# Attention probabilities of even steps: turned by VectorE and a round trip through DRAM instead of by TensorE

## The chip, the cores and the metric

One core of a Trainium2 chip runs the whole program in one launch. The metric is the device time of one execution in microseconds, from the first instruction to the last landing; of several executions the median counts.

## What is computed

The program is one layer: cross-attention with a tanh gate, then a mixture of experts with a tanh gate, both behind a layer norm and both added to `x`. The change lies inside the attention alone. Cut to that (32 sequences of 64 rows, width 512; 32 query heads of 128 in 8 groups that share a key and value head; float32 throughout):

```python
q = rmsnorm((layernorm(x) @ Wq.T).reshape(B, 64, 32, 128), q_norm_w)
k = rmsnorm((ctx @ Wk.T).reshape(B, 64, 8, 128), k_norm_w)      # each shared by 4 query heads
v = (ctx @ Wv.T).reshape(B, 64, 8, 128)
scores = einsum('bhqd,bhkd->bhqk', q, k) / sqrt(128) + mask
probs = softmax(scores)
x = x + tanh(g_xattn) * (einsum('bhqk,bhkd->bhqd', probs, v) @ Wo.T)
```

The product of the probabilities with the values sums over the key positions `k`. TensorE sums over partitions, and the scores come out with the queries on the partitions. So each block of probabilities has to be turned, queries and keys exchanged, before that product.

## The kernel before

**Tiling.** The attention runs in `STEPS` = 64 steps: 8 groups of heads, and in each group 8 steps of 256 rows (4 sequences). A step holds 4 heads x 4 sequences. Its scores are one tile of 128 partitions (2 heads x 64 queries) by 8 blocks of 64 keys. Steps go in pairs; with `i = 2 * d + odd` a step is even or odd, and the two kinds differ in their order of work. Matmuls take float32 numbers as a high part and a rest (`_hi`, `_lo`), three matmuls for one product (`split_product`, L607): the high part is copied out of PSUM by ScalarE, the rest is subtracted by VectorE.

**Who does what in step i.** Each engine has a list of its own, written out by hand, in loops over pairs of steps, and works through it strictly in order; semaphores tie the lists together.

- TensorE (`step`, L777): queries of step i+1 for two halves of the heads (`q_head`, L681); the product of the probabilities of step i-1 with the values (`probs_v`, L731); scores of step i+1 (`scores`, L690); the turn of step i's probabilities (`transpose_probs`, L722: four 128x128 turns against the identity); then the output product of earlier steps (`outputs`, L763, which calls `project_out`, L713, and between its halves `add_quarters`, L708, a small product that completes the sums of the squared queries). In an odd step the turn stands inside the second half of the queries, goes to PSUM banks 2 and 3, and its start is the line `if odd` (L792). In an even step it stands behind the scores (L804) and goes to bank 6. That bank is also written by the first output product, so `outputs` waits there until the turned tile has been read (L771).
- ScalarE (`act_step`, L1201): copies of the queries (`q_out`) and their squares (`squares`), the high part of the turned probabilities (`probs_hi`, L1179), the high part of the attention output (`a_hi_tile`, L1188), the high part of the next group's weight slice (`split_slice`, L1196), and the exponentials of step i+1's softmax (`exps`, L1169).
- VectorE (`dve_step`, L1613): 32x32 block turns and sums of the squared queries (`turn_squares` L1520, `sum_squares` L1529, `split_sums` L1535), the rest of the attention output (`a_rest`, L1513), the rest of the turned probabilities (`probs_lo`, L1589), the softmax of step i+1 (`softmax`, L1544), the addition of the output products into the accumulator (`add_out`, L1506, which stands inside the softmax, while it waits for others), and the rest of the weight slice (`slice_lo`, L1598; for both steps of a pair it stands in the odd one).
- GpSimd: the inverse root of the squared query sums (L500) and the split of the values (`split_v`, L502).
- SP issues the loads (`next_loads`, L370): in each step a slice of 512 columns of weights (L378) and the next values (L384), in each odd step the keys of the next pair (L336). It, too, waits in order.

`softmax` writes the probabilities into the one tile `pb`; its last two passes (L1587) count `p_ready`. The high parts and rests of the turned probabilities go to the tiles `pt`, columns 0 to 127 for even steps and 128 to 255 for odd ones.

The steps 0 to 3 are written out, and so are the last 8 (in the last group other work is mixed in). The loops of the three groups' pairs between them are real loops; each engine jumps back at their ends.

Of the kernel before, what the change touches and what calls it, by code (L numbers as in the profile page):

```python
# [51 lines left out]
STEPS = KVH * NC  # L52
TURNED = (3, STEPS - NC)
# [13 lines left out]
def build(nc, x, ctxT, wk, wv, w_att, w_shd, mask, g_x, g_f, q_w, k_w, gate, w_gu, w_dn, out):  # L67
    kbuf = nc.dram_tensor("kbuf", [STEPS, P, CT], F32, kind="Internal").ap()
    vbuf = nc.dram_tensor("vbuf", [STEPS, P, CT], F32, kind="Internal").ap()
# [3 lines left out]
    k_pair = kbuf.rearrange("(d c) p n -> d p c n", c=2)  # L73
    k_st = kbuf.rearrange("(g c) p (b t) -> c b p g t", g=KVH, b=2)
# [4 lines left out]
    with ExitStack() as ctx:  # L79
# [145 lines left out]
        oh2 = sb("oh2", [P, NT, E])  # L225
        sgt = [sb(f"sgt{q}", [P, D]) for q in range(1)]
# [30 lines left out]
        sq_turned, sq_part, fold_ok = sem("sq_turned"), sem("sq_part"), sem("fold_ok")  # L257
# [10 lines left out]
        tri_ok, rank_out = sem("tri_ok"), sem("rank_out")  # L268
# [17 lines left out]
        dve_mark, pool_mark, ones_ok = sem("dve_mark"), sem("pool_mark"), sem("ones_ok")  # L286
        ctx_first = [sem("ctx_first0"), sem("ctx_first1")]

        block = ctx.enter_context(nc.Block())

# [20 lines left out]
        def _(sp):  # L311

            for s in (v_stored, k_stored, *h2_stored, wgu_last):
                sp.sem_inc(s, 16)
# [55 lines left out]
            def next_loads(d, odd, x_tiles=()):  # L370

                i = 2 * d + odd
                if odd:
                    sp.wait_ge(s_done, i + 1)
                    load_k(d + 1)
                sp.wait_ge(w_hi, i + 8)
# [6 lines left out]
                sp.wait_ge(v_split, 2 * i + 2)  # L383
                sp.dma_start(vt[:].rearrange("p b t -> p (b t)"), vbuf[i + 1]).then_inc(vt_in, 16)  # L384

            with sp.Fori(0, (STEPS - NC) // 2) as d:
                for odd in range(2):
                    next_loads(d, odd)

# [77 lines left out]
        def _(pool):  # L467

            pool.memset(onesb[:], 1.0).then_inc(ones_ok, 1)
            pool.memset(mhalf[:], -0.5).then_inc(pool_const, 1)  # L470
            pool.memset(ident[:], 0.0).then_inc(ident_ok, 1)
            pool.wait_ge(ident_ok, 1)
# [29 lines left out]
            def split_v(j):  # L502
                pool.wait_ge(vt_in, 16 * j + 16)
                pool.wait_ge(pv_done, 2 * j + 2)
                pool.sem_inc(pool_mark, 1)
# [51 lines left out]
            def split_down(z):  # L557
                cs = slice(256 * z, 256 * z + 256)
                pool.wait_ge(shd_in, 16)
                pool.sem_inc(pool_mark, 1)  # L560
# [53 lines left out]
        def _(pe):  # L614
            pe.wait_ge(ones_ok, 1)
            for z in range(WARM):
                pe.matmul(PS[7][:, 0:P], onesb[:], onesb[:], start=(z == 0), stop=(z == WARM - 1))
            pe.wait_ge(ident_ok, 2)
# [144 lines left out]
            def outputs(r, w_before, w_o, o_ready=None, turn=True):  # L763
# [53 lines left out]
            def opening():  # L817
# [29 lines left out]
                pe.wait_ge(fold_ok, 5)  # L847
# [124 lines left out]
            pe.wait_ge(tri_ok, 1)  # L972
# [111 lines left out]
        def _(act):  # L1084
# [94 lines left out]
            def probs_hi(i, odd, bank=2):  # L1179
                act.wait_ge(pT_done, i + 1)  # L1180
# [20 lines left out]
            def act_step(d, odd, w, sl):  # L1201
                i = 2 * d + odd
                act.wait_ge(s_done, i + 1)
                q_out(0, i + 1)
                squares(0, i + 1)
                if odd:
                    probs_hi(i, 1)
# [5 lines left out]
                a_hi_tile(i - 1, 1)  # L1213
                split_slice(i, w, sl)
                exps(i + 1)
# [42 lines left out]
            act.wait_ge(const_dve, 2)  # L1258
# [136 lines left out]
        def _(dve):  # L1395
# [13 lines left out]
            def row_statistics(n, tt):  # L1409
# [3 lines left out]
                dve.sem_inc(dve_mark, 1)  # L1413
# [83 lines left out]
            dve.wait_ge(ident_ok, 2)  # L1497
            dve.tensor_reduce(fold1[:], ident[:].rearrange("p (a j) -> p j a", a=4), AX, ALU.add).then_inc(fold_ok, 1)
            dve.tensor_reduce(quarter[:], ident[:].rearrange("p (a j) -> p a j", a=4), AX, ALU.add).then_inc(fold_ok, 1)
            dve.wait_ge(fold_ok, 2)  # L1500
            dve.tensor_copy(fold[:], fold1[:].unsqueeze(1).to_broadcast([P, 4, 32])).then_inc(fold_ok, 2)
# [42 lines left out]
            def softmax(j, *meanwhile):  # L1544
# [7 lines left out]
                else:  # L1552
                    if j is TURNED[0]:
                        dve.wait_ge(fold_ok, 5)
# [11 lines left out]
                dve.wait_ge(s_done, j + 1)  # L1566
                dve.tensor_tensor(pb[:], PS[3][:].rearrange("p (b s) -> p b s", s=S), per_row(qr),
# [21 lines left out]
            def probs_lo(i, odd, bank=2):  # L1589
                if odd:  # L1590
                    for q in range(2):
                        dve.wait_ge(pT_hi, 2 * i + 1 + q)
                        dve.tensor_tensor(pt_odd(1, q), pT_odd(q, bank), pt_odd(0, q), ALU.subtract).then_inc(pT_evac, 1)
                else:
                    dve.wait_ge(pT_hi, 2 * i + 2)
                    dve.tensor_tensor(pt_even(1), pT_even(), pt_even(0), ALU.subtract).then_inc(pT_evac, 2)
# [16 lines left out]
            def dve_step(d, odd, w, sl, tile_before, tile, complete=(None, None), turn=True):  # L1613

                i = 2 * d + odd
                if turn:
# [15 lines left out]
                if turn and not odd:  # L1632
                    probs_lo(i, 0)
# [10 lines left out]
                softmax(i + 1, while_root, while_exp)  # L1644
# [7 lines left out]
            def opening():  # L1652
# [6 lines left out]
                                quarter[:].unsqueeze(1).unsqueeze(3).to_broadcast([P, 2, 4, 8])).then_inc(fold_ok, 1)  # L1659
# [17 lines left out]
            dve.tensor_copy(trib[:], tri[:]).then_inc(tri_ok, 1)  # L1677
# [5 lines left out]
            dve.wait_ge(const_dve, 2)  # L1683
# [346 lines left out]
```

## Time and profile before

| | us |
|---|---|
| median of 3 runs | 1398.33 (1397.86 to 1398.78) |
| the profiled execution's own time | 1397.51 |
| span of the profiled execution, first to last instruction | 1395.8 |
| TensorE busy | 1382.0 (99%) |
| VectorE busy | 1000.4 (72%) |
| ScalarE busy | 514.6 (37%) |
| GpSimd busy | 358.0 (26%) |
| TensorE's granted clock | 0.999 of 2.4 GHz |

All durations below come from the one profiled execution; its own time is 1.7 us more than its span and lies 0.8 us under the median. In the rows PE is TensorE, PEld its loading of weights, DVE is VectorE, ACT is ScalarE, POOL is GpSimd, SP is the engine that issues the loads. L728 is line 728 of the kernel. Matmuls overlap, so the difference of two starts is a better price than a duration. An engine that is idle costs nothing as long as TensorE isn't.

### The profile page before, as it was taken

How to read it: one execution, taken by the hardware profiler on the slowest of the kernel's cores; microseconds unless marked ns; L12 is line 12 of the kernel's file. 1: busy time of each engine (PE TensorE's matmuls, PEld its weight loads, DVE VectorE, ACT ScalarE, POOL GpSimd, SP SyncE). 2: the span in 40 equal slices, each digit the busy share in tenths (PEclk: the TensorE clock that was granted, in tenths of full speed). 3: DMA queues.
4: the chain of work that ended last, by engine and by line, in shares of the span. 5: the costliest groups of instructions: out<-in, count | busy, mean ns of one | idle time of the engine just before them, and what ended most of it. 6: DMA issues, size and time to landing. Idle time of an engine off the chain costs nothing.

```text
span 1395.8 us, 26753 instructions
## 1 busy us (share of the span) xinstructions
PE 1382.0 (99%) x8757; PEld 1121.7 (80%) x8758; DVE 1000.4 (72%) x2135; ACT 514.6 (37%) x1117; POOL 358.0 (26%) x374
## 2 busy tenths in 40 slices
PE   9999999999999999999999999999999999999998
PEld 7888887888888887888887888888787888777777
DVE  6444456888888888888888888888688746244458
ACT  5333444333333434343333333343434331222242
POOL 1121223221212121212211121212122100367646
PEclk9999999999999999999999999999999999999999
DMA  6544431111111111111101111111123244555548
GB/s 220 189 128 143 128 109 44 39 42 31 49 31 43 39 42 32 43 40 41 43 30 47 36 42 32 49 31 42 54 72 98 99 151 174 188 196 165 165 154 298
DMA packets 91238, 125.52 MB, mean 90 GB/s; under 512 B 7184, under 2 KB 57360, under 8 KB 90896
## 3 DMA queue, kind: packets, MB, share of 16 engines
q1 hardware_dynamic: 83632, 99.70, 22.7%
q0 software_dynamic: 7520, 24.65, 5.3%
q8 instruction: 57, 0.93, 0.3%
q14 instruction: 29, 0.24, 0.1%
HBM read 86.84 MB, written 37.49 MB: 89 GB/s over the span
## 4 chain that ended last, share of the span: by engine, by line
PE 79%; DVE 3%; issue 1%; DMA 1%; ACT 0%; DVEq 0%; POOL 0%; SPq 0%; ACTq 0%
PE ps L609 19%; PE ps L611 18%; PE ps L610 18%; PE ps L1004 6%; PE ps L696 5%; PE ps L743 4%; PE ps L1020 3%; PE ps L728 2%; PE ps L999 1%; DVE acc L1960 1%; DVE acc L1967 1%; DMA y<-ybuf 1%; PE ps L917 1%; PE ps L751 0%; PE ps L1051 0%
## 5 line engine op out<-in xcount | busy, mean ns | idle before, releaser
L506 POOL CAST vth<-vt 128x256 fp32r<-128x256 f32 x64 | 25.4, 397 | 541.4 <-PE ps L743 539.4
L1194 ACT CAST ah<-ps 128x256 fp32r<-128x256 f32 x256 | 83.4, 383 | 187.5 <-PE ps L611 181.0
L609 PE MATMUL ps<-hT,w0h 128*128 128x512 f32 (+1 forms) x384 | 152.2, 396 | 0.0
L611 PE MATMUL ps<-hT,w0h 128*128 128x512 f32 (+1 forms) x384 | 149.9, 390 | 0.0
L610 PE MATMUL ps<-hT,w0l 128*128 128x512 f32 (+1 forms) x384 | 149.6, 390 | 0.0
L500 POOL TENSOR_TENSOR qr<-qv,mhalf 128x8 f32<-128x8 f32 x64 | 105.1, 1642 | 151.5 <-DVE qv L1560 124.3
L1511 DVE TENSOR_TENSOR acc<-ps,acc 128x512 f32 (+1 forms) x128 | 88.0, 687 | 56.6 <-PE ps L611 56.4
L1160 ACT COPY qs<-ps 128x512 f32<-128x512 f32 x128 | 75.3, 588 | 122.6 <-PE ps L611 122.6
L1172 ACT ACTIVATE pb<-pb 128x256 f32<-128x256 f32 x128 | 48.3, 418 | 167.0 <-DVE pb L1578 166.9
L609 PE MATMUL ps<-w0l,ah 128*128 128x512 f32 x256 | 105.6, 413 | 0.0
L609 PE MATMUL ps<-w1l,ah 128*128 128x512 f32 x256 | 104.9, 410 | 0.0
L1517 DVE TENSOR_TENSOR al<-ps,ah 128x256 fp32r<-128x256 f32 x256 | 96.1, 417 | 10.7 <-ACT ah L1194 9.8
L609 PE MATMUL ps<-hT,w1h 128*128 128x512 f32 (+1 forms) x256 | 101.4, 396 | 1.6 <-issue 1.5
L611 PE MATMUL ps<-w0h,ah 128*128 128x512 f32 x256 | 100.3, 392 | 0.0
L611 PE MATMUL ps<-w1h,ah 128*128 128x512 f32 x256 | 100.2, 391 | 0.0
L610 PE MATMUL ps<-w0h,al 128*128 128x512 f32 x256 | 100.0, 391 | 0.0
L611 PE MATMUL ps<-hT,w1h 128*128 128x512 f32 (+1 forms) x256 | 100.0, 391 | 0.0
L610 PE MATMUL ps<-w1h,al 128*128 128x512 f32 x256 | 100.0, 390 | 0.0
L610 PE MATMUL ps<-hT,w1l 128*128 128x512 f32 (+1 forms) x256 | 99.7, 390 | 0.0
L1526 DVE STREAM_TRANSPOSE sqT<-sq 128x512 f32<-128x512 f32 x108 | 76.6, 709 | 29.4 <-ACT sq L1167 24.0
L1004 PE MATMUL ps<-wgu,xgT 128*128 x376 | 94.8, 382 | 0.2 <-issue 0.2
L611 PEld LDWEIGHTS ps<-hT,w0h 128*128 128x128 f32 x384 | 72.1, 188 | 15.3
(250 smaller groups left out, 3216.1 us busy)
## 6 DMA issues: line engine op xcount, KB each, us to landing
wraw<-in_w_att SPq DMA_DIRECT2D x64, 256.0 KB, 2.7
vbuf<-vo SPq DMA_DIRECT2D x16, 512.0 KB, 3.3
kbuf<-ko SPq DMA_DIRECT2D x16, 512.0 KB, 3.8
kt<-kbuf SPq DMA_DIRECT2D x32, 256.0 KB, 2.9
vt<-vbuf SPq DMA_DIRECT2D x64, 128.0 KB, 2.2
wgu<-in_w_gu SPq DMA_DIRECT2D x4, 2048.0 KB, 9.0
y<-ybuf SPq DMA_DIRECT2D x16, 512.0 KB, 7.1
xt<-in_x SPq DMA_DIRECT2D x16, 256.0 KB, 4.2
```

Source lines behind the costliest of these rows:

```text
L500: pool.tensor_tensor(qr[:], qv[:], mhalf[:, 0:8], ALU.pow).then_inc(q_rt, 1)
L609: pe.matmul(dst, l_hi, r_lo, start=first, stop=False)
L610: pe.matmul(dst, l_lo, r_hi, start=False, stop=False)
L611: return pe.matmul(dst, l_hi, r_hi, start=False, stop=last)
L696: mm = pe.matmul(PS[3][h * S:(h + 1) * S, b * S:(b + 1) * S], qs[:, h, b], kt[:, b, :], start=True, stop=True)
L743: mm = pe.matmul(PS[4 + b2][:, bp * 256:(bp + 1) * 256], vhl[v_part][rows, bp, :], pt[p_part][rows, 2 * part + bp, :], start=(z == 0), sto ...
L1004: mm = pe.matmul(PS[2 + q][:, 0:2 * EI], xgT[q][:, k, :], wgu[:, bass.ds(e, 1), k * 2 * EI:(k + 1) * 2 * EI].rearrange("p a n -> p (a n)") ...
L1160: act.copy(qs[:, h].rearrange("p b s -> p (b s)"), PS[h][:]).then_inc(q_copy, 1)
L1194: act.copy(ah[:, bp, :, b2, :], pv_view(bp, b2)).then_inc(a_hi, 1)
L1511: dve.tensor_tensor(dst, PS[6 + bp][:], dst, ALU.add).then_inc(acc_done, 1)
L1517: dve.tensor_tensor(al[:, bp, :, b2, :], pv_view(bp, b2), ah[:, bp, :, b2, :], ALU.subtract).then_inc(a_lo, 1)
L1526: dve.transpose(sqT[:].rearrange("p n i -> p (n i)"), sq[:, h].rearrange("p b s -> p (b s)")).then_inc(sq_turned, 1)
```

## The change

In the even steps 4 to 54 (26 steps, `BY_DMA`) TensorE no longer turns the probabilities.

- VectorE turns the tile in blocks of 32x32 at the start of the step, into a tile `pbT`. This exchanges queries and keys within each block, but the blocks stay on the wrong partitions.
- SP writes `pbT` to DRAM (256 KB), waits for it to land, and reads it back with four loads of 64 KB, one for each 32 partitions, into the tile `pt_raw`; the addresses put the blocks into place. In an even step SP's order becomes: wait for the block turn and for the last read back, store; weight slice; wait for the store, four loads; values.
- ScalarE's `probs_hi` of such a step reads `pt_raw` instead of PSUM, and stands behind `split_slice` and ahead of `exps`; it waits for the four loads.
- VectorE's `probs_lo` of such a step also reads `pt_raw`, and moves from ahead of the softmax of step i+1 to behind it. `slice_lo` stays where it is.
- `outputs` of such a step doesn't wait for the turned tile any more, as bank 6 isn't used for it.

Some semaphores are joined, with the counts moved accordingly, and SP's loop starts at step 4. The two new tiles lie where two tiles of the last group lie, so SP waits once behind its loop until the last of them is read.

```diff
+BY_DMA = (4, STEPS - NC)
...
+    pbuf = nc.dram_tensor("pbuf", [P, 4, P], F32, kind="Internal").ap()
...
+    p_ld = pbuf.rearrange("(q j) c n -> c j q n", q=4)
...
+            pbT = sb("pbT", [P, 4, 4, 32], F32, a)
+            pt_raw = sb("pt_raw", [P, 4, 4, 32], F32, a)
...
+        def by_dma(i, odd):
+            return not odd and (not isinstance(i, int) or BY_DMA[0] <= i < BY_DMA[1])
...
+            def next_loads(d, odd, x_tiles=(), k=None):
                 i = 2 * d + odd
+                if k is not None:
+                    sp.wait_ge(p_turned, k + 1)
+                    sp.wait_ge(p_back, 64 * k + 64)
+                    sp.dma_start(pbuf, pbT[:].rearrange("p c m i -> p c (m i)")).then_inc(p_out, 16)
                 if odd:
                     sp.wait_ge(s_done, i + 1)
                     load_k(d + 1)
                 sp.wait_ge(w_hi, i + 8)
                 sp.wait_ge(w_lo, i + 8)
                 sp.dma_start(wraw[:], w_att[i + NC]).then_inc(wr_in, 16)
...
+                    if k is not None:
+                        probs_back(k)
+                    sp.wait_ge(v_split, 2 * i + 2)
+                    sp.dma_start(vt[:].rearrange("p b t -> p (b t)"), vbuf[i + 1]).then_inc(vt_in, 16)
+            def probs_back(k):
+                sp.wait_ge(p_out, 16 * k + 32)
+                sp.wait_ge(pT_evac, 4 * k + 6)
+                for c in range(4):
+                    sp.dma_start(pt_raw[32 * c:32 * c + 32].rearrange("p q m i -> p q (m i)"),
+                                 p_ld[c]).then_inc(p_back, 16)
...
             def outputs(...):
-                pe.wait_ge(pT_evac, 2 * r + 4)
+                if not bank_free:
+                    pe.wait_ge(pT_evac, 2 * r + 4)
...
             def step(...):
-                if not odd:
+                dma = turn and by_dma(i, odd)
+                if not odd and not dma:
                     pe.wait_ge(acc_done, 2 * i)
                     transpose_probs(i, odd)
-                outputs(i - 1, w_before, w_o, o_ready, turn)
+                outputs(i - 1, w_before, w_o, o_ready, turn, dma)
...
+            def probs_hi(i, odd, bank=2, d=None):
+                if by_dma(i, odd):
+                    act.wait_ge(p_back, 64 * d)
+                    act.wait_ge(pv_done, 2 * i + 2)
+                    act.copy(pt_even(0).rearrange("p m (q i) -> p q m i", q=4), pt_raw[:]).then_inc(pT_hi, 2)
+                    return
...
             def act_step(d, odd, w, sl):
                 a_hi_tile(i - 1, 0)
-                if not odd:
+                if not odd and not by_dma(i, odd):
                     probs_hi(i, 0)
                 a_hi_tile(i - 1, 1)
                 split_slice(i, w, sl)
+                if by_dma(i, odd):
+                    probs_hi(i, 0, d=d)
                 exps(i + 1)
...
             def dve_step(...):
+                if by_dma(i, odd):
+                    dve.wait_ge(p_ready, 2 * i + 2)
+                    dve.wait_ge(p_out, 16 * (d - 1))
+                    dve.transpose(pbT[:].rearrange("p c m i -> p (c m i)"),
+                                  pb[:].rearrange("p (m z) (h j) -> p (z h) m j", z=2, h=2)).then_inc(p_turned, 1)
                 if turn:
                     turn_squares(i + 1, 0)
...
-                if turn and not odd:
+                if turn and not odd and not by_dma(i, odd):
                     probs_lo(i, 0)
...
-                softmax(i + 1, while_root, while_exp)
+                softmax(i + 1, while_root, while_exp, turn_before=d - 1 if by_dma(i, odd) else None)
+                if by_dma(i, odd):
+                    probs_lo(i, 0)
                 if odd or not turn:
                     slice_lo(i, w, sl)
```

## Rows read from the trace of the kernel before

**Rows 1.** The page, its part 1: busy time, share of the span, instructions.

```profile
PE 1382.0 (99%) x8757; PEld 1121.7 (80%) x8758; DVE 1000.4 (72%) x2135; ACT 514.6 (37%) x1117; POOL 358.0 (26%) x374
```

**Rows 2.** Busy time by engine, steps 4 to 55; last clock, DMA share, GB/s.

```profile
255.26:968.84 713.58, 711.38 (x5046) 582.85 (x5044) 609.70 (x1329) 273.29 (x651) 143.78 (x156) 1.00 0.14 39
```

**Rows 3.** Waits of the same stretch: us in total, times, longest us.

```profile
ACT pth L1186 <- PE ps L728: 28.0, 26, 1.1
...
DVE sqT L1526 <- issue: 4.6, 2, 2.5
...
PE ps L710 <- DVE sqs_hl L1542: 0.6, 1, 0.6
```

**Rows 4.** TensorE's timeline, an even and an odd step: start us, us.

```profile
597.74 1.15 PE L696 MATMUL ps<-kt,qs 128*64 128x64 f32 x32
...
604.94 0.39 PE L609 MATMUL ps<-hT,w1h 128*128 x1
...
609.02 0.60 PE L728 MATMUL ps<-ident,pb 128*128 128x128 f32 x4
...
610.95 0.39 PE L743 MATMUL ps<-ptl,vth 64*128 64x256 f32 x2
...
611.85 1.15 PE L696 MATMUL ps<-kt,qs 128*64 128x64 f32 x32
612.93 0.50 PE L609 MATMUL ps<-w1l,ah 128*128 128x512 f32 x1
...
614.42 0.19 PE L710 MATMUL ps<-sqs_hl,fold 128*128 128x64 f32 x1
...
618.64 0.39 PE L609 MATMUL ps<-hT,w1h 128*128 128x512 f32 x1
```

**Rows 5.** VectorE's timeline, the same two steps; in brackets idle before, releaser.

```profile
595.87 0.70 DVE L1526 STREAM_TRANSPOSE sqT<-sq 128x512 f32<-128x512 f32 x1
...
598.07 0.71 DVE L1526 STREAM_TRANSPOSE sqT<-sq 128x512 f32<-128x512 f32 x1 [0.78 <-ACT sq L1167]
...
599.76 0.19 DVE L1542 TENSOR_TENSOR sqs_hl<-sqs,sqs_hl 128x32 fp32r<-128x32 f32 x1
...
600.55 0.68 DVE L1596 TENSOR_TENSOR ptl<-ps,pth 128x512 fp32r<-128x512 f32 x1
601.15 0.28 DVE L1555 SCALAR_TENSOR_TENSOR ssg<-ps,quarters 128x64 f32<-128x64 f32 x1
...
602.55 0.69 DVE L1511 TENSOR_TENSOR acc<-ps,acc 128x512 f32 x1 [0.86 <-PE ps L611]
...
608.21 0.76 DVE L1587 TENSOR_TENSOR pb<-pb,rc 128x256 f32<-128x256 f32 x2
...
610.07 0.76 DVE L1593 TENSOR_TENSOR ptl<-ps,pth 128x256 fp32r<-128x256 f32 x2 [0.38 <-ACT pth L1183]
...
612.18 0.71 DVE L1526 STREAM_TRANSPOSE sqT<-sq 128x512 f32<-128x512 f32 x1 [0.16 <-ACT sq L1167]
...
616.25 0.69 DVE L1511 TENSOR_TENSOR acc<-ps,acc 128x512 f32 x1 [1.07 <-PE ps L611]
```

**Rows 6.** ScalarE's timeline, the even step: weight slice, exponentials.

```profile
603.08 0.63 ACT L1198 CAST w0h<-wraw 128x512 f32 x1
606.44 0.75 ACT L1172 ACTIVATE pb<-pb 128x256 f32<-128x256 f32 x2 [2.74 <-DVE pb L1578]
```

**Rows 7.** Landings of the 16 stores of 256 KB to h2buf.

```profile
DMA to landing us min/median/max: 2.0/2.5/3.5
```

**Rows 8.** Landings of the 64 loads of 128 KB into vt.

```profile
DMA to landing us min/median/max: 1.9/2.2/3.8
```

**Rows 9.** SP's timeline, the even step: weight slice, values, keys.

```profile
596.16 0.33 SPq L378 DMA_DIRECT2D wraw<-in_w_att  x1
599.40 0.33 SPq L384 DMA_DIRECT2D vt<-vbuf  x1
599.99 0.38 SPq L336 DMA_DIRECT2D kt<-kbuf  x1
```

More of the change, by code:

```diff
@@ L225, in build @@
         oh2 = sb("oh2", [P, NT, E])
+        with ExitStack() as a:
+            pbT = sb("pbT", [P, 4, 4, 32], F32, a)
+            pt_raw = sb("pt_raw", [P, 4, 4, 32], F32, a)
         sgt = [sb(f"sgt{q}", [P, D]) for q in range(1)]
@@ L283, in build, with pT_before @@
         y_scaled = sem("y_scaled")
-        dve_mark, pool_mark, ones_ok = sem("dve_mark"), sem("pool_mark"), sem("ones_ok")
+        mark = sem("mark")
+        p_turned, p_out, p_back = sem("p_turned"), sem("p_out"), sem("p_back")
         ctx_first = [sem("ctx_first0"), sem("ctx_first1")]
         block = ctx.enter_context(nc.Block())
+        def by_dma(i, odd):
+            return not odd and (not isinstance(i, int) or BY_DMA[0] <= i < BY_DMA[1])
+        def pT_before(i, d):
+            if not isinstance(i, int):
+                return d + 2
+            return i if i < BY_DMA[0] else i - (BY_DMA[1] - BY_DMA[0]) // 2
         def turned(j):
@@ L311, in _ @@
         def _(sp):
-            for s in (v_stored, k_stored, *h2_stored, wgu_last):
+            for s in (v_stored, k_stored, p_out, *h2_stored, wgu_last):
                 sp.sem_inc(s, 16)
@@ L382, in next_loads @@
                     sp.dma_start(xt3[n % 2][:], x[n]).then_inc(x3_in[n % 2], 16)
-                sp.wait_ge(v_split, 2 * i + 2)
-                sp.dma_start(vt[:].rearrange("p b t -> p (b t)"), vbuf[i + 1]).then_inc(vt_in, 16)
-            with sp.Fori(0, (STEPS - NC) // 2) as d:
+                if not False:
+                    if k is not None:
+                        probs_back(k)
+                    sp.wait_ge(v_split, 2 * i + 2)
+                    sp.dma_start(vt[:].rearrange("p b t -> p (b t)"), vbuf[i + 1]).then_inc(vt_in, 16)
+            def probs_back(k):
[4 more added lines that the diff above has]
+                                 p_ld[c]).then_inc(p_back, 16)
+            sp.sem_inc(p_back, 64)
+            for d in range(BY_DMA[0] // 2):
                 for odd in range(2):
                     next_loads(d, odd)
+            with sp.Fori(0, (BY_DMA[1] - BY_DMA[0]) // 2) as k:
+                next_loads(k + BY_DMA[0] // 2, 0, k=k)
+                next_loads(k + BY_DMA[0] // 2, 1)
+            sp.wait_ge(pT_evac, 2 * BY_DMA[1] - 2)
             for t in range(NC - 1):
@@ L504, in split_v @@
                 pool.wait_ge(pv_done, 2 * j + 2)
-                pool.sem_inc(pool_mark, 1)
+                pool.sem_inc(mark, 1)
                 pool.tensor_copy(vhl[0][:], vt[:]).then_inc(v_split, 1)
@@ L559, in split_down @@
                 pool.wait_ge(shd_in, 16)
-                pool.sem_inc(pool_mark, 1)
+                pool.sem_inc(mark, 1)
                 pool.tensor_copy(dn_hi[:, cs], dn_raw[:, cs]).then_inc(shd_hi, 1)
@@ L614, in _ @@
         def _(pe):
-            pe.wait_ge(ones_ok, 1)
+            pe.wait_ge(ident_ok, 1)
             for z in range(WARM):
                 pe.matmul(PS[7][:, 0:P], onesb[:], onesb[:], start=(z == 0), stop=(z == WARM - 1))
-            pe.wait_ge(ident_ok, 2)
+            pe.wait_ge(ident_ok, 3)
             pe.sem_inc(ss_done, 1)
@@ L761, in gate_up_half, with outputs @@
                     mm.then_inc(gu_done, 1)
-            def outputs(r, w_before, w_o, o_ready=None, turn=True):
+            def outputs(r, w_before, w_o, o_ready=None, turn=True, bank_free=False):
                 pe.wait_ge(acc_done, 2 * r + 1)
@@ L846, in opening @@
                 scores(1, 1)
-                pe.wait_ge(fold_ok, 5)
+                pe.wait_ge(const_dve, 6)
                 pe.wait_ge(acc_done, 4)
@@ L970, in _ @@
             gate_up(1, 3)
-            pe.wait_ge(tri_ok, 1)
+            pe.wait_ge(const_dve, 7)
             pe.wait_ge(rank_in, 1)
@@ L1177, in _ @@
                 squares(h, 0)
-            def probs_hi(i, odd, bank=2):
-                act.wait_ge(pT_done, i + 1)
+            def probs_hi(i, odd, bank=2, d=None):
[4 more added lines that the diff above has]
+                    return
+                act.wait_ge(pT_done, pT_before(i, d) + 1)
                 if odd:
@@ L1206, in act_step @@
                 if odd:
-                    probs_hi(i, 1)
+                    probs_hi(i, 1, d=d)
                 q_out(1, i + 1)
@@ L1210, in act_step @@
                 a_hi_tile(i - 1, 0)
-                if not odd:
+                if not odd and not by_dma(i, odd):
                     probs_hi(i, 0)
                 a_hi_tile(i - 1, 1)
+                if by_dma(i, odd) and False:
+                    probs_hi(i, 0, d=d)
                 split_slice(i, w, sl)
+                if by_dma(i, odd):
+                    probs_hi(i, 0, d=d)
                 exps(i + 1)
@@ L1257, in _ @@
             act.wait_ge(g_in, 16)
-            act.wait_ge(const_dve, 2)
+            act.wait_ge(const_dve, 8)
             act.copy(g_hl[:, :, 0:E], graw[:].rearrange("p (k e) -> p k e", k=KD)).then_inc(g_hi_ok, 1)
@@ L1412, in row_statistics @@
                 dve.wait_ge(ln_st, n + 1)
-                dve.sem_inc(dve_mark, 1)
+                dve.sem_inc(mark, 1)
                 dve.bn_aggr(mv1[:], st1[:]).then_inc(ln_mv, 1)
@@ L1496, in _ @@
                         kv_tile(2 * m + cp, 4 * m + 2 * cp + tt, cp, tt)
[L1497 to L1501, printed above, removed]
+            dve.wait_ge(ident_ok, 3)
+            dve.tensor_reduce(fold1[:], ident[:].rearrange("p (a j) -> p j a", a=4), AX, ALU.add).then_inc(const_dve, 1)
+            dve.tensor_reduce(quarter[:], ident[:].rearrange("p (a j) -> p a j", a=4), AX, ALU.add).then_inc(const_dve, 1)
+            dve.wait_ge(const_dve, 3)
+            dve.tensor_copy(fold[:], fold1[:].unsqueeze(1).to_broadcast([P, 4, 32])).then_inc(const_dve, 2)
             for n in range(NT - 4, NT):
@@ L1542, in split_sums, with softmax @@
                 dve.tensor_tensor(sqs_hl[:, 1, :], flat, sqs_hl[:, 0, :], ALU.subtract).then_inc(sq_part, 1)
-            def softmax(j, *meanwhile):
+            def softmax(j, *meanwhile, turn_before=None):
                 per_row = lambda t: t[:].unsqueeze(2).to_broadcast([P, 8, S])
@@ L1566, in softmax @@
                 dve.wait_ge(s_done, j + 1)
+                if turn_before is not None:
+                    dve.wait_ge(p_turned, turn_before)
                 dve.tensor_tensor(pb[:], PS[3][:].rearrange("p (b s) -> p b s", s=S), per_row(qr),
@@ L1595, in probs_lo @@
                     dve.wait_ge(pT_hi, 2 * i + 2)
+                    if by_dma(i, odd):
+                        dve.tensor_tensor(pt_even(1).rearrange("p m (q i) -> p q m i", q=4), pt_raw[:],
+                                          pt_even(0).rearrange("p m (q i) -> p q m i", q=4),
+                                          ALU.subtract).then_inc(pT_evac, 2)
+                        return
                     dve.tensor_tensor(pt_even(1), pT_even(), pt_even(0), ALU.subtract).then_inc(pT_evac, 2)
@@ L1642, in while_exp @@
                     add_out(2 * i, 0, tile)
-                softmax(i + 1, while_root, while_exp)
+                softmax(i + 1, while_root, while_exp, turn_before=d - 1 if by_dma(i, odd) else None)
+                if by_dma(i, odd):
+                    probs_lo(i, 0)
                 if odd or not turn:
```

18 lines of the change are left out of this document (9 added, 9 removed).

## The prediction

> **What bounds the kernel now.** First the busy shares: TensorE is busy for 99% of the span [rows 1]. Then the stretch that the change touches, steps 4 to 55, from their first scores to those of step 56: 713.58 us, TensorE busy 711.38 of them at the full granted clock of 1.00 (2.4 GHz), VectorE 609.70, ScalarE 273.29 [rows 2]. So VectorE is 85% full and has (713.58 - 609.70) / 26 = 4.0 us without work in each pair of an even and an odd step. Then the waits of that stretch: TensorE waits for VectorE once, 0.6 us; VectorE stands twice, 4.6 us in all, with nothing to wait for ("issue"), and the row of ScalarE's copies says that even turns happen 26 times [rows 3]. TensorE goes from one matmul to the next; what leaves its list comes off the time, if nothing else becomes late.
>
> **What leaves TensorE.** The price is read from starts, since its matmuls overlap. In an even step the scores start at 597.74 and the next step's first query product at 604.94, with the four turns between: 7.20 us. The odd step, whose turns lie elsewhere, has the same work between 611.85 and 618.64: 6.79 us [rows 4]. The difference, 0.41 us, is what four turns cost, a mode switch included (the 0.60 us of the row at 609.02 is no price, since its end lies under the next matmul). 26 x 0.41 = 10.7 us. The wait of `outputs` for VectorE's rest of the probabilities (line 771) goes too; nothing shows that it ever held TensorE: 0.
>
> The Trainium skill (VectorE: DVE Perf Modes, The three transpose paths) gives TensorE 390 ns for a 128x128 turn in bf16 and VectorE 311 ns, for 32x32 blocks only, and its rules for kernel authors choose TensorE where PSUM may be the goal, as here. By 390 ns four turns would be 1.56 us and the sum 40.6 us; the trace says 0.41 us, as they stream one behind the other, and the trace decides.
>
> **What VectorE gets.** One more 128x512 block turn in each even step. The trace has that operation on another tile, 0.70 to 0.71 us [rows 5]; the new one reads runs of 32 numbers out of order, so I bound it by 0.6 (what one such pass adds between its neighbours, 600.55 to 601.15) and 1.4 us (twice the row), and take 0.71, the same instruction on the same size. It stands at the head of the step, at 595.87 in the clock of these rows, and pushes the first turn of the squares to 596.61. There the cover is visible: before the second turn of squares, at 598.07, VectorE sits idle for 0.78 us, waiting for ScalarE's squares [rows 5]. 0.72 goes into 0.78: 0 on the path.
>
> The rest of the probabilities (`probs_lo`, 600.55, one pass of 0.60) moves behind the softmax. The even step's chain then starts 0.60 sooner on VectorE, but add_out waits for TensorE at 602.55 already (0.86 us idle) [rows 5]; so the chain starts when TensorE lets it, 0.41 earlier than today, and ends 0.41 earlier, at 608.97 - 0.41 = 608.56. TensorE's odd turns come at 609.02 - 0.41 = 608.61 [rows 4], so they meet the same small margin as now. Then `probs_lo` takes 0.60, and the turn of squares, which follows p_ready at once today, starts at 609.17, 0.60 late against TensorE. The idle 0.38 before the odd rest at 610.07 and 0.16 before the turn at 612.18 take up 0.54 of it [rows 5]: the odd rest starts at about 609.17 + 0.73 = 609.90, 0.24 late against TensorE; its first half is done at 610.32, and TensorE's product with the values, which waits for it, stands at 610.95 - 0.41 = 610.54 [rows 4]. 0.22 us are left. The second turn of squares comes at 611.76, where its squares let it start anyway (612.18 - 0.41). The sums for add_quarters, ready at 599.95 in the even step [rows 5], are wanted at 597.74 + 2.57 = 600.31, the distance from the scores that the odd step shows (611.85 to 614.42) [rows 4]. So 0 again, with thin covers: the 0.22 is the first to go.
>
> **The round trip.** The turn ends at 596.58. SP then stores (p_turned), loads the weight slice (it moves from 596.16 to about 597.2, and ScalarE takes it at 603.08, 5.9 us later: covered), waits for the store, issues four loads, and only then v (599.40) and, in the odd step, k (599.99) [rows 6, 9]. Store: nearest row, 256 KB to DRAM, 2.0 / 2.5 / 3.5 us, I take 2.5 [rows 7]. Loads of 64 KB: nearest row 128 KB, 1.9 / 2.2 / 3.8, I take 2.2 [rows 8]. Issues 0.33 to 0.38 with some 0.07 between them [rows 9]. Issue 596.8, landed 599.3, four issues 599.5 to 600.7 (start of the last), landed 602.9. v and k leave some 1.6 us later, at 601.1 and 601.6; v is split only after the product at 610.5 and k first read by the scores at 611.4: over 9 us for each, where the longest landing of v is 3.8 [rows 8]: covered.
>
> ScalarE waits for the loads behind its weight slice (603.08, 0.63 us) and ahead of the exponentials (606.44) [rows 6]; all of that 0.41 earlier it is at the wait from 603.2 and must begin its copy (a pass like the slice's) by 606.03 - 0.63 = 605.4. So the trip, expected at 602.9, has 2.5 us to spare; it would cost nothing from below, and from above, with landings of 3.5 and 3.8 us [rows 7, 8] and issues twice as long as the 0.38 seen, it ends at 596.8 + 3.5 + 0.2 + 3 x 0.83 + 3.8 = 606.8, 1.4 too late. I take 0: the traffic in this stretch is low (39 GB/s, [rows 2]), so the usual landings are the nearest.
>
> **Where VectorE is late already.** Twice in this stretch, behind the end of a loop body, it stands for about 2.3 us (the 4.6 above), and once TensorE waits 0.6 us for it [rows 3]. There the idle 0.78 doesn't exist, so the new turn's 0.5 to 0.7 and TensorE's 0.41 both show: about 0.9 at the one place, 0.2 at the other: +1.0. Where that standing time moves with the changed code I can't tell; what is there now gives 0 to 2.5 us either way.
>
> **Sum.** -10.7 + 1.0 = -9.7. Against the profiled execution, 1397.5 us (span 1395.8 and 1.7 around it), 1387.8; that execution lies 0.8 under the median of the runs, so 1388.6. The other stages hold the same work: 0.
>
> **The rivals.**
> (a) The trip is late. The place is ScalarE's in-order list: its wait stands ahead of the exponentials, VectorE's sum waits for these, and TensorE's odd turns for the result, with 0.05 us to spare now. It decides from 8.8 us after the turn on (596.6 to 605.4), and makes the kernel slower than today once it is 0.41 us later still. With the upper rows: 1.4 x 26 - 9.7 = +26.7, some 1425 us. For it: slow rows exist, at other times. Against it: the usual rows come to 6.3 us. In this direction speaks also a trap of the same section of the Trainium skill: a plain DMA that turns by its strides is 19 times slower than the DMA crossbar when its innermost stride is large; no run here shows one, and here each piece is a run of 512 bytes. Chance 0.11.
> (b) VectorE gives part back. Its thin places (0.22 at the product with the values, 0.05 at the odd turns) don't hold: a wait costs more than a row shows, or the turn runs over 0.71. If the 0.24 comes through in each pair, 6.2 us are lost: about 1395; half of it, 1392. Chance 0.16, still faster.
> (c) The gain is taken up. TensorE is early, but the softmax chain isn't, and TensorE waits 0.41 at each odd turn: 1398, no change. Against it: the chain's first link waits for TensorE (0.86 and 1.07 idle at 602.55 and 616.25) [rows 5]. Chance 0.06.
>
> **How the numbers follow.** My forecast 0.67, (a) 0.11, (b) 0.16, (c) 0.06. A measurement of this kernel tells 0.2%, 2.8 us, from no change. Faster: 0.67 + 0.16 = 0.83; same 0.06; slower 0.11. The range goes from 1386.3 (all of 10.7, and a little of the standing time gone) to 1396, the upper end of (b).
>
> **What would show it.** Right: the distance from an even step's scores to the next step's first query product is 6.8 instead of 7.2 us; 26 fewer groups of turns on TensorE; VectorE's idle 0.78 before the second turn of squares is gone; the last of the four loads lands before ScalarE reaches its copy. Wrong: ScalarE idle ahead of that copy until after 605.4 in this clock, TensorE waiting at the odd turns or at the product with the values in most pairs, or a turn of the probabilities well above 0.71 us.

## The result, and the profile after

The changed kernel takes 1389.7 us (median of 4 runs, 1387.83 to 1390.29) where the kernel before takes 1398.27 (4 runs on the same chip): a ratio of 0.9936, 95% interval 0.9919 to 0.9953. The profiled execution took 1387.83 us against 1397.51, 9.7 less, with a span of 1386.1. The forecast was 1388.6, range 1386.3 to 1396.

Busy shares of the changed kernel, the page's part 1. Against [rows 1] TensorE has 104 matmuls fewer, which is 26 x 4, and VectorE 26 instructions more.

```profile
PE 1373.1 (99%) x8653; PEld 1112.3 (80%) x8654; DVE 1012.3 (73%) x2161; ACT 512.9 (37%) x1117; POOL 359.8 (26%) x374
```

The stretch from the first scores of step 4 to those of step 56, busy time by engine as in [rows 2]: 704.84 us instead of 713.58, so 8.74 of the 9.7 come from here. VectorE has only (704.84 - 620.80) / 26 = 3.2 us without work in a pair, instead of 4.0.

```profile
254.89:959.73 704.84, 701.63 (x4942) 572.78 (x4941) 620.80 (x1355) 271.64 (x651) 144.07 (x156) 1.00 0.20 59
```

TensorE's timeline (start, us), an even and an odd step, as in [rows 4]:

```profile
593.80 1.15 PE L737 MATMUL ps<-kt,qs 128*64 128x64 f32 x32
...
596.38 0.19 PE L751 MATMUL ps<-sqs_hl,fold 128*128 128x64 f32 x1
...
600.59 0.39 PE L650 MATMUL ps<-hT,w1h 128*128 x1
...
604.67 0.60 PE L769 MATMUL ps<-ident,pb 128*128 128x128 f32 x4
...
607.50 1.15 PE L737 MATMUL ps<-kt,qs 128*64 128x64 f32 x32
...
614.31 0.39 PE L650 MATMUL ps<-hT,w1h 128*128 128x512 f32 x1
...
620.74 1.15 PE L737 MATMUL ps<-kt,qs 128*64 128x64 f32 x32
```

From scores to the next query product the even step now takes 600.59 - 593.80 = 6.79 us, the odd one 6.81: the 0.41 us of [rows 4] is gone. The step of 13.70 us between two scores was 14.11 (611.85 - 597.74 in [rows 4]). A steady pair, from the scores of one even step to those of the next, takes 26.94 us (620.74 - 593.80) instead of 27.33 (625.07 - 597.74, with this row of before):

```profile
625.07 1.15 PE L696 MATMUL ps<-kt,qs 128*64 128x64 f32 x32
```

VectorE's timeline for the same steps (in brackets the idle time before, and what ended it), as in [rows 5]:

```profile
591.31 0.68 DVE L1660 TENSOR_TENSOR w0l<-wraw,w0h 128x512 f32 x1
591.91 0.70 DVE L1678 STREAM_TRANSPOSE pbT<-pb 128x512 f32<-128x512 f32 x1
592.54 0.67 DVE L1578 STREAM_TRANSPOSE sqT<-sq 128x512 f32<-128x512 f32 x1
...
594.12 0.71 DVE L1578 STREAM_TRANSPOSE sqT<-sq 128x512 f32<-128x512 f32 x1 [0.19 <-ACT sq L1210]
...
595.81 0.19 DVE L1594 TENSOR_TENSOR sqs_hl<-sqs,sqs_hl 128x32 fp32r<-128x32 f32 x1
...
598.22 0.69 DVE L1563 TENSOR_TENSOR acc<-ps,acc 128x512 f32 x1 [1.08 <-PE ps L652]
...
604.55 0.68 DVE L1651 TENSOR_TENSOR ptl<-pt_raw,pth 128x512 fp32r<-128x512 f32 x1
```

The block turn pushes the next instruction back by 0.63 us (591.91 to 592.54), and the idle 0.78 of [rows 5] has shrunk to 0.19. The sums of the squares are ready at 596.00 (595.81 + 0.19), and TensorE takes them at 596.38.

The round trip, SP's timeline (first three rows) and ScalarE's (last two):

```profile
592.74 0.33 SPq L393 DMA_DIRECT2D pbuf<-pbT  x1
593.40 0.33 SPq L404 DMA_DIRECT2D wraw<-in_w_att  x1
594.80 1.75 SPq L419 DMA_DIRECT2D pt_raw<-pbuf  x4
...
599.26 0.63 ACT L1226 CAST pth<-pt_raw 128x512 fp32r<-128x512 f32 x1
...
602.11 0.75 ACT L1215 ACTIVATE pb<-pb 128x256 f32<-128x256 f32 x2 [2.21 <-DVE pb L1632]
```

The turn ends at 592.61. The store is issued at 592.74 and has landed when the loads begin (594.80); of all 104 loads the landings are in the next row, and the last one here landed at 598.10. ScalarE copies at 599.26 with no idle time before, and then waits 2.21 us for VectorE.

```profile
DMA to landing us min/median/max: 1.8/1.9/3.0
```

The waits of the stretch (us in total, times, longest), as in [rows 3], and the first of the two places where VectorE stands behind the end of a loop body, with what TensorE waits there:

```profile
DVE pbT L1678 <- issue: 4.4, 2, 2.2
...
PE ps L751 <- DVE sqs_hl L1594: 3.0, 2, 1.7
```

```profile
538.30 0.71 DVE L1678 STREAM_TRANSPOSE pbT<-pb 128x512 f32<-128x512 f32 x1 [2.24 <-issue]
```

```profile
542.38 0.30 PE L751 MATMUL ps<-sqs_hl,fold 128*128 128x64 f32 x1 [1.74 <-DVE sqs_hl L1594]
```

VectorE stands as long as before (4.4 against 4.6 us), but TensorE now waits 3.0 us for it instead of 0.6. Another row is gone: in the kernel before, TensorE also stood once by itself, waiting for nothing that the profile shows, and that was at the second of the two places. The first two rows are of the kernel before, the third shows the second place after:

```profile
PE ps L609 <- issue: 1.5, 1, 1.5
```

```profile
756.89 0.49 PE L609 MATMUL ps<-hT,w1h 128*128 128x512 f32 x1 [1.46 <-issue]
```

```profile
759.89 0.30 PE L751 MATMUL ps<-sqs_hl,fold 128*128 128x64 f32 x1 [1.29 <-DVE sqs_hl L1594]
```

Before, the pause of 1.46 us gave VectorE time at the second place: the sums were ready at 765.65, and TensorE took them at 766.41. After, the pause is missing, and TensorE waits 1.29 us for VectorE instead. From scores to scores the two pairs that hold the loop ends take 28.67 and 29.08 us before, 28.99 and 28.95 after. Over their steady pairs (27.33 and 26.94) that is 3.1 us before and 4.1 after.

### The profile page after: what moved, and what is told of

Read it like the earlier page. It is cut to its first block, busy times and chain, and to the rows that moved or that the text cites. A ratio compares the mean times of both kernels' runs of the same rounds, so it can differ in the third digit from the quotient of the medians.

```text
span 1386.1 us, 26799 instructions
## 1 busy us (share of the span) xinstructions
PE 1373.1 (99%) x8653; PEld 1112.3 (80%) x8654; DVE 1012.3 (73%) x2161; ACT 512.9 (37%) x1117; POOL 359.8 (26%) x374
## 4 chain that ended last, share of the span: by engine, by line
PE 77%; DVE 4%; issue 2%; DMA 1%; ACT 0%; DVEq 0%; POOL 0%; ACTq 0%
PE ps L650 19%; PE ps L652 18%; PE ps L651 18%; PE ps L1047 6%; PE ps L737 5%; PE ps L784 4%; PE ps L1063 3%; PE ps L1042 1%; PE ps L769 1%; DVE acc L2026 1%; DVE acc L2033 1%; PE ps L960 1%; PE ps L792 0%; DVE sqs L1584 0%; DVE sqT L1578 0%
## 5 line engine op out<-in xcount | busy, mean ns | idle before, releaser
L652 PEld LDWEIGHTS ps<-hT,w0h 128*128 128x128 f32 x384 | 72.1, 188 | 15.3
L650 PEld LDWEIGHTS ps<-hT,w0h 128*128 128x128 f32 x384 | 72.1, 188 | 15.2 <-issue 0.8
```

The source lines that it names most:

```text
L650: pe.matmul(dst, l_hi, r_lo, start=first, stop=False)
L652: return pe.matmul(dst, l_hi, r_hi, start=False, stop=last)
```

## The experiments

All but the last are edits of the changed kernel, and all are compared with the kernel before on the same chip (a to d on one chip, e to h on another, i on a third). The changed kernel's own ratio, 0.9936, makes it 1388.9 us on the chip of a to d and 1388.6 on that of e to h.

| run | median us (runs) | ratio, 95% interval |
|---|---|---|
| a, TensorE's turns kept | 1397.23 (10) | 0.9998, 0.9989 to 1.0008 |
| b, no turn and no trip | 1386.97 (5) | 0.9925, 0.9911 to 0.9939 |
| c, block turn twice | 1403.51 (5) | 1.0042, 1.0028 to 1.0056 |
| d, loads in two parts | 1388.40 (4) | 0.9933, 0.9918 to 0.9949 |
| e, loads in a chain | 1414.38 (4) | 1.0137, 1.0104 to 1.0169 |
| f, odd steps too | 1473.32 (4) | 1.0550, 1.0521 to 1.0579 |
| g, VectorE's loop written out | 1384.72 (4) | 0.9910, 0.9894 to 0.9927 |
| h, f and g together | 1469.79 (4) | 1.0519, 1.0502 to 1.0537 |
| i, kernel before, loop written out | 1398.31 (11) | 1.0006, 0.9997 to 1.0015 |

### a. TensorE keeps four turns

```diff
+                if dma:
+                    pe.wait_ge(acc_done, 2 * i)
+                    for m in range(4):
+                        pe.transpose(PS[6][:, m * P:(m + 1) * P], ident[:], ident[:])
                 outputs(i - 1, w_before, w_o, o_ready, turn, dma)
```

> The changed kernel, but TensorE again does four 128x128 turns at the old place of the 26 even steps, of a constant tile that nothing reads (the probabilities still come by VectorE and DRAM). Theory (TensorE sets the pace and 0.39 to 0.41 us per even step was all that the change bought): the pair of steps goes from 26.94 back to about 27.33 us, and the time from 1389.7 to some 1399 us, as before the change. Rival (the gain came from the wait that went, or from the shorter list of ScalarE and VectorE around the turn): no more than 2 us come back, 1390 to 1392 us.

Measured: 1397.23 us, the time of before. A steady pair takes 27.31 us again (27.33 before, 26.94 after), in these rows 625.25 - 597.94:

```profile
597.94 1.15 PE L737 MATMUL ps<-kt,qs 128*64 128x64 f32 x32
...
625.25 1.15 PE L737 MATMUL ps<-kt,qs 128*64 128x64 f32 x32
```

So the gain is the four turns on TensorE; the other parts of the change together give nothing.

### b. No turn, no trip

```diff
-                if k is not None:
-                    sp.wait_ge(p_turned, k + 1)
-                    sp.wait_ge(p_back, 64 * k + 64)
-                    sp.dma_start(pbuf, pbT[:]...)
...
-                    if k is not None:
-                        probs_back(k)
...
+            pool.memset(pt_raw[:].rearrange("p q m i -> p (q m i)"), 0.0)
...
-                    act.wait_ge(p_back, 64 * d)
+                    act.wait_ge(acc_zero, 2)
...
-                if turn_before is not None:
-                    dve.wait_ge(p_turned, turn_before)
...
-                if by_dma(i, odd):
-                    ...
-                    dve.transpose(pbT[:]..., pb[:]...).then_inc(p_turned, 1)
```

> The changed kernel without VectorE's block turn, the store and the four loads: the high part and rest are taken from a tile of zeros, so the even steps' probabilities are left out of the result. Theory (turn and trip lie under other work except at the two places where VectorE stands at the end of a loop body): 1 to 2 us faster than the changed kernel, 1388 us, and the pair of steps stays at 26.92 to 26.94 us. Rival (VectorE's extra turn gives part of the gain back in each pair, 0.1 to 0.24 us): 3 to 6 us faster, 1384 to 1387 us, pair 26.7 to 26.85.

Measured: 1386.97 us, 1.9 less than the changed kernel by the medians and 0.9 less between the profiled executions. The steady pair is 26.94 us in both, so the turn and its trip cost nothing there; VectorE's idle time is back in the row:

```profile
593.78 0.71 DVE L1573 STREAM_TRANSPOSE sqT<-sq 128x512 f32<-128x512 f32 x1 [0.79 <-ACT sq L1205]
```

What it gains lies at the loop ends, where TensorE's waits for VectorE's sums fall from 3.0 to 2.2 us in all, and in the one pair where VectorE also sets up two constants ahead of its loop (27.30 us in the changed kernel, 26.94 here).

### c. The block turn twice

```diff
                     dve.wait_ge(p_out, 16 * (d - 1))
+                    dve.transpose(pbT[:]..., pb[:]...).then_inc(p_turned, 1)
+                    dve.wait_ge(p_turned, 2 * d - 3)
                     dve.transpose(pbT[:]..., pb[:]...).then_inc(p_turned, 1)
...
```

The counts that SP and the softmax wait for are moved accordingly.

> The changed kernel with VectorE's block turn done twice in each of the 26 even steps, the second behind the first. Theory (behind one turn the cover is 0.19 us of idle time ahead of the second turn of squares, and the sums then have some 0.35 us before TensorE wants them): of the second turn's 0.65 to 0.75 us about 0.1 to 0.2 comes through to TensorE per pair and the whole of it at the two loop ends: 4 to 7 us slower than the changed kernel, 1394 to 1397 us, TensorE waiting ahead of the product that completes the sums in all 26 even steps. Rival (a turn is fully on the path): 17 to 19 us slower, 1407 us. Rival (VectorE has room anyway): under 1.5 us, 1390 to 1391.

Measured: 1403.51 us, 14.6 more than the changed kernel, between the theory (4 to 7) and the first rival (17 to 19). VectorE's and TensorE's rows in one even step:

```profile
599.23 0.68 DVE L1660 TENSOR_TENSOR w0l<-wraw,w0h 128x512 f32 x1
599.91 0.71 DVE L1678 STREAM_TRANSPOSE pbT<-pb 128x512 f32<-128x512 f32 x1
600.65 0.71 DVE L1681 STREAM_TRANSPOSE pbT<-pb 128x512 f32<-128x512 f32 x1
601.29 0.67 DVE L1578 STREAM_TRANSPOSE sqT<-sq 128x512 f32<-128x512 f32 x1
...
602.81 0.71 DVE L1578 STREAM_TRANSPOSE sqT<-sq 128x512 f32<-128x512 f32 x1
```

```profile
601.72 1.15 PE L737 MATMUL ps<-kt,qs 128*64 128x64 f32 x32
...
604.74 0.30 PE L751 MATMUL ps<-sqs_hl,fold 128*128 128x64 f32 x1 [0.28 <-DVE sqs_hl L1594]
```

From the rest of the weight slice to the first turn of squares VectorE takes 2.06 us instead of 1.23, 0.83 more. Of the idle 0.19 only 0.06 absorbs any (1.52 us between the two turns of squares instead of 1.58; 0.12 between a sum and the next turn stays where nothing waits for ScalarE). Some 0.33 more goes into the 0.38 that the sums had ahead of TensorE. The rest arrives: the small product stands 3.02 us behind the scores instead of 2.58, 0.44 late, and 26 x 0.44 = 11.4 us. The stretch takes 14.3 us more (719.18 instead of 704.84), and of the 2.9 that remain the two loop ends give 2.6. So the cover that the prediction counted on was real, and it is nearly used up: of an addition at VectorE's head, what goes beyond 0.4 us arrives at TensorE.

### d, e. The loads in two parts, and one by one

```diff
                 for c in range(4):
+                    if c in (2,):            # e: (1, 2, 3)
+                        sp.wait_ge(p_back, 64 * k + 64 + 16 * c)
                     sp.dma_start(pt_raw[32 * c:32 * c + 32]..., p_ld[c]).then_inc(p_back, 16)
```

> The changed kernel, but SP issues the third load back only when the first two have landed, so the trip is about 1.5 to 2 us longer: the last landing moves from 598.1 to some 600 in the clock of the step whose scores start at 593.8, and the latest time for ScalarE is 601.5. Theory (only the deadline counts): no change, 1389.7 within 1 us, though ScalarE now waits for the loads by up to 0.8 us. Rival (the trip is on the path already): 26 times 1.5 to 2, 40 to 50 us slower, 1430 us and more.

> The changed kernel, but SP issues each of the four loads back only when the one before has landed. With the loads in two pairs the last landing came 5.6 us after the even step's scores; three more waits for a landing instead of one put it at about 8.5. ScalarE must begin its copy 7.7 us after the scores at the latest. Theory (a deadline): some 0.8 us late in each pair, so about 20 us slower than the changed kernel (1388.5 in the last session), 1405 to 1415 us, ScalarE waiting for the loads in every pair and its exponentials late. Rival (there is further room behind that deadline): no change, 1388 to 1390 us.

Measured: d 1388.40 us, no change; e 1414.38, 26 more than the changed kernel. In d the four issues stretch over 3.12 us instead of 1.75; ScalarE now waits for the loads, a little, and still has 1.94 us to spare ahead of the exponentials:

```profile
595.51 3.12 SPq L421 DMA_DIRECT2D pt_raw<-pbuf  x4
...
600.25 0.62 ACT L1228 CAST pth<-pt_raw 128x512 fp32r<-128x512 f32 x1 [0.18 <-DMA pt_raw<-pbuf]
...
602.82 0.76 ACT L1217 ACTIVATE pb<-pb 128x256 f32<-128x256 f32 x2 [1.94 <-DVE pb L1634]
```

In e (SP's, ScalarE's and VectorE's rows of one even step, and TensorE's turn) the four issues stretch over 5.86 us, and the spare time is gone:

```profile
608.30 5.86 SPq L421 DMA_DIRECT2D pt_raw<-pbuf  x4
```

```profile
615.79 0.62 ACT L1228 CAST pth<-pt_raw 128x512 fp32r<-128x512 f32 x1 [2.93 <-DMA pt_raw<-pbuf]
616.31 0.72 ACT L1217 ACTIVATE pb<-pb 128x256 f32<-128x256 f32 x2
...
617.06 0.69 DVE L1638 TENSOR_REDUCE sm<-pb 128x8 f32<-128x512 f32 x1 [0.56 <-ACT pb L1217]
...
618.50 0.77 PE L771 MATMUL ps<-ident,pb 128*128 128x128 f32 x4 [0.18 <-DVE pb L1643]
```

With the scores of this step at 607.29, the odd turns stand 11.21 us behind them instead of 10.87 (604.67 - 593.80 after). That is rival (a): ScalarE's copy, then the exponentials, VectorE's sum, TensorE's turns. Even steps take from 14.1 to 15.7 us here instead of 13.70, and 16.5 and 16.6 at the loop ends. The stretch takes 728.43 us instead of 704.84, 23.6 more, of the 24.4 between the profiled executions.

The fixed part is what makes a chain dear. In the changed kernel loads of 64, 128 and 256 KB (`pt_raw`, `vt`, `wraw`) land in 1.9, 2.1 and 2.6 us and the store of 256 KB in 2.0. So four times the bytes cost 0.7 us more at most, and three landings in a chain take most of 5.86 us. The Trainium skill (DMA: Bandwidth & Descriptors, Anatomy of one DMA) puts the fixed cost of a DMA at about 2.0 us and adds a price for the bytes, for transfers that GpSimd issues; the 1.9 us of SP's smallest loads agree with that fixed cost here.

### f, h. The odd steps too

```diff
-            return not odd and (not isinstance(i, int) or BY_DMA[0] <= i < BY_DMA[1])
+            return not isinstance(i, int) or BY_DMA[0] <= i < BY_DMA[1]
...
-                next_loads(k + BY_DMA[0] // 2, 1)
+                next_loads(k + BY_DMA[0] // 2, 1, k=k)
...
+                    if by_dma(i, odd):
+                        slice_lo(i - 1, w if w_last is None else w_last, ...)
```

> The odd steps 5 to 55 go the same way as the even ones (52 round trips); the rest of a step's weight slice moves to the next step's idle time ahead of the first addition of the output product, the rest of the turned probabilities stands behind each softmax, and SP issues the weight slice last. Theory (what leaves TensorE comes off the time as long as VectorE's head of a step fits before the product that completes the sums: an odd step's head then has the length of an even one's, with about 0.4 us to spare): TensorE's pair goes from 26.94 to about 26.46 us, 26 x 0.48 = 12.5 us, less what the two loop ends take back: 1376 to 1379 us. Rival (VectorE, 24.7 us busy per pair, becomes the bound): the pair stays above 26.7, 1383 us or more.

> The kernel that turns all steps from 4 to 55 by VectorE and DRAM, with VectorE's outer loop written out as well. Theory: both gains add up, 1388.5 - 12.5 - 3 = 1373 us, 1372 to 1376. Rival (VectorE is the bound with odd steps too, and its standing only moves): 1380 us or more.

Measured: 1473.32 and 1469.79 us. The theory of each missed (1376 to 1379 and 1372 to 1376); the rivals, 1383 or more and 1380 or more, hold by the number, but not by their cause, VectorE as the bound. The runs don't test what they were made for. As built, the product with the values reads the columns of both steps of a pair in one go, so those of the odd step are not yet its own, and the result is another one. And the time is set elsewhere. In f's waits TensorE stands longest for the keys, whose load comes behind the odd step's store in SP's list:

```profile
PE ps L739 <- DMA kt<-kbuf: 58.6, 25, 2.9
```

The granted clock of that stretch is 0.95 in the mean. Whether VectorE could carry the odd turns too, with the product a step later and the keys loaded first, stays open: it wasn't tried. h is 3.5 us under f, about what g gives alone (3.9).

### g, i. VectorE's loop over the groups written out

```diff
-            with dve.Fori(0, KVH // 2 - 1) as gg:
+            for gg in range(KVH // 2 - 1):
```

i is the same edit in the kernel before.

> The changed kernel with VectorE's outer loop over three pairs of groups written out, so that VectorE doesn't jump back over a long body. Theory (the 2.2 us that VectorE stands at two loop ends are the loading of its code behind the jump, and TensorE's waits of 1.7 and 1.3 us there come from it): both waits go, 2.5 to 3.5 us faster than the changed kernel, 1385 to 1386 us. Rival (the code has to be loaded anyway, and VectorE stands elsewhere): within 1 us of the changed kernel, 1388 to 1390 us.

> The kernel before with VectorE's loop over the groups written out, as in g_unrolled. Theory: before the change VectorE's standing behind the end of its loop body was almost covered by its idle 0.78 us; only some 0.7 us of waiting at TensorE came from it, so the time falls by 0.7, and by up to 1.6 more if TensorE's own pause at 755.0 goes as well: 1395.2 to 1396.8 us. Then the change is worth 10.5 to 12 us between the two kernels without VectorE's loop, more than the 9.7 with it. Rival: the written-out loop gives the same 3.5 to 4 us whatever else the kernel does (as less code to load, or fewer jumps): about 1393.7, and the change is worth 9 to 9.7 in both forms.

Measured: g 1384.72 us, about 4 less than the changed kernel and 0.991 of the kernel before: the fastest of all. The steady pair is the same, 26.94. The rows of VectorE standing for "issue" are gone from g's waits, and of TensorE's waits for the sums this is left:

```profile
PEld ps L751 <- DVE sqs_hl L1594: 0.4, 1, 0.4
```

i: 1398.31 us, no change that can be told: the kernel before took 1397.63 on that chip, the ratio is 1.0006. The median lies above the theory's 1395.2 to 1396.8, which only the profiled execution meets, 1396.19, the fastest of its 11; the rival's 1393.7 falls. VectorE no longer stands, but TensorE's own pause, which was 1.5 us long in the trace of before, is still there, now at the first loop end:

```profile
536.87 0.49 PE L609 MATMUL ps<-hT,w1h 128*128 128x512 f32 x1 [1.40 <-issue]
```

So VectorE's jump back cost the kernel before next to nothing, as its idle time and, at the second place, TensorE's own pause covered most of it, and it costs the changed kernel 4 us. Between the two forms without that loop the change is worth 1396.19 - 1384.46 = 11.7 us by the profiled executions, and some 13 by the two ratios (1.0006 and 0.9910). Of the 11.7, 10.1 are the steady pairs and 1.4 TensorE's pause, which neither g's trace shows nor that of the changed kernel. Why it is missing there was not found. In the two traces that have it, two packets of the instruction queue 8 start close together ahead of it (between 752.3 and 753.0 us before, 532.3 and 533.0 in i); at the other loop end of each trace there is one. That the two belong together is not shown.

## Why the prediction was right

**TensorE's price.** Right: 0.41 us for the four turns, taken from starts, is what the even step lost (7.20 to 6.79), and a, which puts the turns back, takes the time of before again. The odd step grew by 0.02, so a pair won 0.39 and 26 pairs 10.1 us, instead of 10.7.

By the 390 ns that the Trainium skill (VectorE: DVE Perf Modes, The three transpose paths) gives for one turn in bf16 on TensorE, 40.6 us should have gone, as an estimate; 10.1 went. The trap of the same section, a plain DMA that turns by its strides, doesn't show here: the loads, in runs of 512 bytes, landed in 1.9 us. The preference of the page's rules for kernel authors, TensorE where PSUM may be the goal, did not hold here, where TensorE sets the time and VectorE and the DMA queues have room.

**VectorE's turn.** Right that 0.78 us of idle time covers it: b shows the pair unchanged without it. It took 0.63 where 0.72 was allowed for. c shows how much was left: 0.06 and some 0.33.

**The rest of the probabilities behind the softmax.** Right: no wait of TensorE for VectorE or ScalarE at the product with the values or at the odd turns stands in the waits after. Rival (b) did not happen in any steady pair. The 0.36 us named for the sums (599.95 to 600.31 in [rows 4, 5]) is 0.38 now.

**The round trip.** Right, with room: from the end of the turn to the last landing 5.5 us (592.61 to 598.10) instead of 6.3, as the store landed in 2.0 and not 2.5, and the loads in 1.9 and not 2.2. The copy could have begun 2.21 us later, at 601.47, so 3.4 us were to spare and not 2.5. d uses 1.4 of them (3.12 - 1.75) and loses nothing, e uses all and loses 26 us. The place where rival (a) decides is as the prediction had it, and the point within half a us: in e's rows the copy begins 8.50 us behind the scores, 0.83 over the latest time of 7.67 (601.47 - 593.80), and the turns are 0.34 late. The usual landings were the ones to take.

**The loop ends.** The number was right: 3.1 us over the steady pairs before and 4.1 after, 1.0 more, as forecast. The mechanism was right at the first place, where the wait for VectorE went from 0.6 to 1.74 us (1.15 more, forecast 0.9). At the second the forecast of 0.2 was met by luck: the wait for VectorE grew from 0 to 1.29 us, while TensorE's own pause of 1.46 us, which the prediction left out although it stands in the waits of the stretch before, went away. g shows that the standing of VectorE is what the waits hang on. What the prediction didn't see is that the change turned a harmless pause into one that costs 4 us and can be removed.

**The sum.** -9.7 forecast, -9.7 measured between the profiled executions, but by terms that make up for one another: -10.1 in the pairs, +1.0 at the loop ends, +0.4 in the one pair where VectorE sets up its constants, and about -0.9 outside the stretch, which no step explains. The profiled execution is the lowest of four runs, and by the medians the change is worth 8.6 us. Rival (c) fell: the odd turns follow the scores without a wait.

## What to carry to other kernels

When one engine is busy for 99% of the span, take its work away in the engine's own price, the difference between starts with and without it, and pay with resources that have idle time: a trip through DRAM of 5.5 us is free where 8.9 us lie between maker and taker. Before adding work to an engine, look at the idle time at that very place, and not at its share: VectorE kept 3.2 us free in each pair and still had room for only 0.4 more at the head of the step. And look where the pattern breaks: pauses at loop ends that were covered before come out when the cover is spent, and writing the loop out brought 4 us more.

## What was not expected of the hardware

**VectorE stands 2.2 us behind a far jump back.** Between its last instruction of the loop body and the first of the next, with nothing to wait for (2.24 and 2.18 us). Written out, the pause is gone, and the profile page's count of instruction packets on queue 14 falls from 29 to 24 (0.24 to 0.19 MB). In the changed kernel one such packet of 8 KB falls into each of the two pauses, some 0.2 us behind their start; the DMA view of 535.9 to 538.5 us has nothing else:

```profile
q14 instruction: 1, 0.01, 1.0%
```

The packet takes some 0.4 us, and why the pause lasts 2.2 is open. That it is code being loaded is likely by this, but no run shows it.

**The clock fell after one wait of 2.4 us, and not after one of 2.6.** In c, TensorE waited at both loop ends:

```profile
548.36 0.30 PE L751 MATMUL ps<-sqs_hl,fold 128*128 128x64 f32 x1 [2.37 <-DVE sqs_hl L1594]
...
771.45 0.30 PE L751 MATMUL ps<-sqs_hl,fold 128*128 128x64 f32 x1 [2.57 <-DVE sqs_hl L1594]
```

These windows show its busy time and granted clock before the first wait, just behind it, and later, and then just behind the second:

```profile
540.00:545.50 5.50, 5.50 (x60) 1.00 0.01 3
548.50:552.00 3.50, 3.50 (x10) 0.51 0.55 165
553.00:556.00 3.00, 3.00 (x15) 1.00 0.00 0
...
771.50:775.00 3.50, 3.50 (x16) 1.00 0.59 159
```

Behind the first wait the clock is 0.51, the lower level (1.2 GHz), with matmuls 0.43 us apart instead of 0.23, and then 1.00 again. Behind the second, 0.2 us longer, it stays at 1.00, so the length of the wait alone does not decide. The pair of the first loop end takes 31.63 us, that of the second 29.83. In the changed kernel, with waits of 1.74 and 1.29 us at the same places, the clock stayed at 1.00. A wait can so cost more than its length.
